# Linear attention with routed experts: kv and the sum of k in one product per two heads, scatters spread over the batch on GpSimd, which also squares the k values

## What is computed

```python
h = layernorm(x) * (1 + ca) + sa
def feature_map(x, orf):                       # x: a head's 8 values, orf: (32, 8)
    proj = x @ orf.T / d_k ** 0.25
    norm = sum(x * x, -1) / (2 * sqrt(d_k))
    return (exp(proj - norm) + EPS) / sqrt(m)  # EPS = 1e-6
q, k = feature_map(h @ Wq.T + bq), feature_map(h @ Wk.T + bk);  v = h @ Wv.T + bv
kv = einsum('nlm,nld->nmd', k, v);  ksum = sum(k, axis=1)
out = (q @ kv) / (q @ ksum)
x = x + ga * (out @ Wo.T + bo)
h = layernorm(x) * (1 + cb) + sb
top1 = argmax(h @ gate_W + gate_b)
x = x + gb * (gelu(h @ W1[top1] + b1[top1]) @ W2[top1] + b2[top1])
```

## Time and profile before

| | us |
|---|---|
| median of three runs | 385.43 (384.46 to 388.31) |
| the profiled execution | 384.86, span 383.1 |
| PE busy in the span | 363.1 (95%) |
| PE weight loads | 281.6 (74%) |
| ACT busy | 278.2 (73%) |
| DVE busy | 271.2 (71%) |
| POOL busy | 202.1 (53%) |

### The profile page before, as it was taken

How to read it: one execution, slowest core, us unless ns; L and a number is a source line. 1 busy time by engine, 2 the same in 40 slices (tenths; PEclk the granted TensorE clock), 3 DMA queues, 4 the chain that set the end, 5 groups by cost and what they waited for, 6 DMA issues and landing times.

```text
span 383.1 us, 13102 instructions
## 1 busy us (share of the span) xinstructions
PE 363.1 (95%) x4547; PEld 281.6 (74%) x4547; DVE 271.2 (71%) x1128; ACT 278.2 (73%) x720; POOL 202.1 (53%) x226
## 2 busy tenths in 40 slices
PE   8899999999999999999999978999989999999990
PEld 7465765766576575657657647999989998999990
DVE  4626787887878779778676879787677775666660
ACT  2588888788888878888888747766656665666650
POOL 2131454854674565657537546546767554555552
PEclk9999999999999999999999999999999999999997
DMA  6496745721321222232122247544565666545310
GB/s 218 175 314 262 248 187 171 226 81 63 113 87 51 93 86 71 74 111 81 47 103 86 71 136 233 159 122 134 167 194 177 188 209 174 165 127 145 89 32 0
DMA packets 30783, 52.38 MB, mean 137 GB/s; under 512 B 4194, under 2 KB 22758, under 8 KB 30336
## 3 DMA queue, kind: packets, MB, share of 16 engines
q1 hardware_dynamic: 24352, 34.50, 30.0%
q0 software_dynamic: 6368, 17.05, 12.2%
HBM read 28.46 MB, written 19.34 MB: 125 GB/s over the span
## 4 chain that ended last, share of the span: by engine, by line
PE 78%; DVE 4%; SPq 3%; issue 3%; ACT 3%; POOL 3%; DMA 3%; DVEq 1%; POOLq 0%; ACTq 0%
PE ps_proj L1247 11%; PE ps_proj L1051 8%; PE ps_feat L1234 6%; PE ps_proj L1084 4%; PE ps_kv L1099 4%; PE ps_feat L1070 4%; PE ps_den L1117 4%; PE ps_kv L1103 4%; PE ps_kv L1131 3%; PE ps_out L1056 3%; PE ps_proj L1087 3%; PE ps_kv L1121 3%; PE ps_feat L1073 3%; PE ps_den L1234 3%; PE ps_kv L1234 3%
## 5 line engine op out<-in xcount | busy, mean ns | idle before, releaser
L484 POOL DMA_INDIRECT out<-kf,modb x71 | 70.7, 995 | 57.3 <-DVE kf L977 50.4
L1247 PE MATMUL ps_proj<-w2sb,qf 128*128 x568 | 74.8, 275 | 0.0
L451 POOL DMA_INDIRECT experts_lists<-pay,slot x64 | 63.8, 997 | 19.1 <-issue 17.4
L1247 PEld LDWEIGHTS ps_proj<-w2sb,qf 128*128 128x128 f32 x568 | 68.9, 192 | 0.2 <-issue 0.2
L613 ACT ACTIVATE xT<-ps_out 128x128 f32<-128x128 f32 x71 | 19.7, 278 | 47.3 <-PE ps_out L1227 47.3
L972 DVE TENSOR_TENSOR kf<-ps_proj,firsts_sb 128x128 f32<-128x128 f32 x71 | 20.7, 291 | 36.2 <-PE ps_proj L1247 25.0
L438 POOL TENSOR_TENSOR wo<-wsb,modb 128x128 f32<-128x128 f32 x16 | 7.6, 475 | 69.2 <-ACT den L591 69.2
L621 ACT ACTIVATE qf<-ps_feat,shared 128x128 f32<-128x128 f32 x144 | 41.0, 376 | 0.0
L1234 PE MATMUL ps_feat<-xT,shared 128*128 128x128 f32 x288 | 38.7, 277 | 1.7 <-issue 0.6
L1234 PEld LDWEIGHTS ps_feat<-xT,shared 128*128 128x128 f32 x288 | 35.0, 192 | 2.9 <-issue 1.6
L1051 PE MATMUL ps_proj<-shared,wsb 128*128 128x512 f32 x62 | 33.4, 620 | 0.3 <-ACT shared L521 0.3
(11 more groups left out here) (187 smaller groups left out, 982.4 us busy)
## 6 DMA issues: line engine op xcount, KB each, us to landing
modb<-experts_lists SPq DMA_DIRECT2D x71, 196.0 KB, 2.5
xall<-in_x SPq DMA_DIRECT2D x16, 256.0 KB, 4.4
pay<-modb SPq DMA_DIRECT2D x16, 256.0 KB, 2.7
modb<-modulation_rows SPq DMA_DIRECT2D x1, 3072.0 KB, 12.1
firsts_sb<-in_firsts SPq DMA_DIRECT2D x1, 2576.0 KB, 10.2
experts_lists<-padding SPq DMA_DIRECT2D x9, 196.0 KB, 2.3
out<-kf,modb POOLq DMA_INDIRECT x71, 2.7
modb<-modulation_rows SPq DMA_DIRECT2D x1, 1024.0 KB, 6.0
```

The lines of the kernel that those rows point to most:

```text
L451: g_.indirect_dma_start(out=lists, in_=pay[b.home][:, t, :], in_offset=None, out_offset=bass.IndirectOffsetOnAxis(ap=slot[b.home][:, t:t + ...
L484: g_.indirect_dma_start(out=rows_out, in_=yb[u], in_offset=None, out_offset=bass.IndirectOffsetOnAxis(ap=token, axis=0), bounds_check=last ...
L1247: ins = mm(Y[u % 2][:, 0:D], g[u % R4][:, c * P:(c + 1) * P], w2sb[:, bass.ds(e * DFF + c * D, D)], start=(c == 0), stop=(c == FC - 1))
```

## The change

- kv and the sum of k come out of one product. The features are laid out by pairs of heads, `kf[:, t, c, j, 0:64]` with the EPS column behind each 64. The stationary operand `v1` has 32 columns for group c and pair j: 16 of v and 16 ones. There are 32 matmuls of 65 columns instead of 16 of 129 and 16 of 128.
- kvT has 128 columns instead of 256 (mask and products 64 wide), so there is one transpose. kvm is copied in two halves of 64 partitions onto a tile that was zeroed.
- kveps is made by TensorE (eight matmuls of one column, ahead of the den product, into bank F[0]) and copied by VectorE between `centre_h2` and `scale_h2`. `k_features` of the next batch waits for that copy, since it writes the same bank.
- ScalarE no longer squares the k values (but for batch 0) and normalises two tiles of each batch; VectorE normalises the other two. `modulate` stands one activation earlier, `k_values` behind `kvm_copy`.
- GpSimd squares the k values (`k_squares(b+1)`), between tile 3 of the scatter of batch b-3 and tile 0 of that of b-2. `gated(b)` follows, then tiles 1 and 2; tile 3 is left for the next batch.

```diff
@@ GpSimd @@
+            g_.memset(kvm[:], 0.0).then_inc(s_kvz, 1)
+            g_.memset(v1[:, :, CW // 2:CW], 1.0).then_inc(s_kvz, 1)
...
+            def k_squares(b):
+
+                pool.wait_ge(s_kst, b.v + 1)
+                g_.tensor_tensor(ksqs, kvals, kvals, ALU.mult).then_inc(s_ksq, 1)
+
...
                 if ahead and b.par == 0:
                     rstd1_of(b.half + 3, b=b + 2)
+                if b.v >= 3:
+                    scatter(b + -3, (3,))
+                if not last:
+                    k_squares(b + 1)
+                if not first and not second:
+                    scatter(b + -2, (0,))
                 gated(b, first)
                 if not first and not second:
-                    scatter(b + -2)
+                    scatter(b + -2, (1, 2))
+                if last:
+                    scatter(b + -2, (3,))
@@ ScalarE @@
             def kvm_copy(b):
                 act.wait_ge(s_kvt, b.v + 1)
-                a.activation(kvm[:], G[:, 0:2 * P], ACT.Copy).then_inc(s_kvm, 1)
+                if b.v == 0:
+                    act.wait_ge(s_kvz, 2)
+                for j in range(2):
+                    half = slice(j * HP, (j + 1) * HP)
+                    a.activation(kvm[half, :, :, j, :], G[half, 0:P].rearrange("p (c n i) -> p n c i", c=NC, n=2),
+                                 ACT.Copy).then_inc(s_kvm, 1)
...
                 k_feature(b, 3)
-                if not first and not last:
-                    normalise1(b + 1, LT // 2, LT)
...
                 q_feature(b, 1)
-                q_feature(b, 2)
                 if not last:
                     modulate(b + 1)
+                q_feature(b, 2)
                 q_feature(b, 3)
+                kvm_copy(b)
                 if not last:
                     k_values(b + 1)
-                kvm_copy(b)
-                if not last:
-                    k_squares(b + 1)
                     q_parts(b + 1)
@@ VectorE @@
-                v.scalar_tensor_tensor(out=kvT[:, 0:P], in0=KV[:, 0:P], scalar=KV[:, P:P + 1], in1=mask,
-                                       op0=ALU.add, op1=ALU.mult, accum_out=kvsum[:, 0:1])
-                v.scalar_tensor_tensor(out=kvT[:, P:2 * P], in0=KV[:, 256:256 + P], scalar=float(L * FEPS), in1=mask,
-                                       op0=ALU.add, op1=ALU.mult, accum_out=kvsum[:, 1:2]).then_inc(s_kvT, 1)
-                dve.wait_ge(s_kvT, b.v + 1)
-                v.tensor_scalar(kveps[:], kvsum[:], FEPS, None, ALU.mult).then_inc(s_eps, 1)
+                for j in range(2):
+                    at = j * (HP + 1)
+                    ins = v.scalar_tensor_tensor(out=kvT[:, j * HP:(j + 1) * HP], in0=KV[:, at:at + HP],
+                                                 scalar=KV[:, at + HP:at + HP + 1], in1=mask,
+                                                 op0=ALU.add, op1=ALU.mult)
+                ins.then_inc(s_kvT, 1)
+
+            def eps_values(b):
+
+                dve.wait_ge(s_epsp, b.v + 1)
+                if b.v:
+                    dve.wait_ge(s_oT, b.v)
+                v.tensor_copy(kveps[:], F[0][:, 0:2]).then_inc(s_eps, 1)
...
+                if not first and not last:
+                    normalise1(b + 1, lo=LT // 2)
                 if not first:
                     residual(b + -1)
                     second_stats(b + -1)
...
                     centre_h2(b + -1)
+                eps_values(b)
+                if not first and not last:
                     scale_h2(b + -1)
@@ TensorE @@
-                pe.wait_ge(s_kst, 2 * (b.v + 1))
+                pe.wait_ge(s_kst, b.v + 1)
+                pe.wait_ge(s_ksq, b.v + 1)
                 if not first:
+                    pe.wait_ge(s_eps, b.v)
...
-                for t in range(LT):
-                    for c in range(NC):
-                        mm(KV[c * CW:(c + 1) * CW, 0:P + 1], v_sb[:, t, c * CW:(c + 1) * CW], kf[:, t, c, 0:P + 1],
-                           start=(t == 0), stop=(t == LT - 1))
-                for t in range(LT):
-                    for c in range(NC):
-                        ins = mm(KV[c * CW:(c + 1) * CW, 256:256 + P], ones32[:], kf[:, t, c, 0:P],
-                                 start=(t == 0), stop=(t == LT - 1))
+                for j in range(2):
+                    for t in range(LT):
+                        for c in range(NC):
+                            ins = mm(KV[c * CW:(c + 1) * CW, j * (HP + 1):(j + 1) * (HP + 1)],
+                                     v1[:, (t * NC + c) * 2 + j, :], kf[:, t, c, j, :],
+                                     start=(t == 0), stop=(t == LT - 1))
                 ins.then_inc(s_kv, 1)
...
+                kv = kvm[:, :, :, :, :].rearrange("p n c j i -> p n c (j i)")
+                for n in range(2):
+                    for c in range(NC):
+                        ins = mm(F[0][c * CW:(c + 1) * CW, n:n + 1], kv[:, n, c, :], kf[:, 0, 0, 0, HP:HP + 1],
+                                 start=True, stop=True)
+                ins.then_inc(s_epsp, 1)
```

68 lines of the change are left out of this document (36 added, 32 removed).

## The result

The changed kernel takes **392.59 us** (median of four runs, 391.52 to 395.26) where the kernel before took 386.32 beside it (384.46 to 388.31): ratio 1.0206, 95% interval 1.0166 to 1.0247. That is slower, clear of the noise, by 1.7 to 2.5 per cent, and by nearly the amount forecast: +7.85 on the profiled execution was predicted (392.7), and the profiled executions stand 6.7 apart (391.52 for 384.86; span 389.7 for 383.1).

A forecast was written before the change was run, and what follows sets the result against it. TensorE, busy throughout 60 to 195, was taken as the bound. With VectorE fully blocked, −0.65 − 0.75 + 4.2 + 5.05 = +7.85 on the profiled 384.86 gave 392.7 us; range 381 to 397.

The forecast's parts named there:

- The product: TensorE's batch: one kv product of about 1.02 replaces the kv product (1.02) and the product with the ones (0.87), gaining 0.87.
- hT: ScalarE's modulation, one activation earlier, ends near 141.5, later than the shorter kv product needs: 0.13 charged per batch.
- The unblocked batch: TensorE's batch if nothing is late: 13.48 − 0.87 − 0.13 + 0.12 + 0.13 = 12.73; whole kernel 381.3, chance 0.25.
- The rival that the product doesn't shrink: 64 loads and passes limit the kv product to 1.9; batch 13.6 without blocking, kernel about 390, or 400 blocked; chance 0.05.
- Full blocking: GpSimd's squares keep VectorE's two-SBUF-input operations out, 0 to 1.28 a batch; batch 13.8, kernel 392.7, chance 0.45.
- the odd batch: Batch without first_moments, with VectorE blocked: centre_h2 ends 1.28 later, k_features 0.82 late, out_project 0.24 more; batch 13.79.
- The even batch: Batch with first_moments: blocked squares end near A+3.05 (A: TensorE starts the attention products), 1.1 late; batch 13.83.
- Start of the batches: Batch 0 gains 0.65 and the interval behind it, without centre_h2, 0.75; 13 more lose 0.32 each.
- The late tile: Tile 3 of batch 12, moved behind rstd2 of batch 14, delays the first expert block's load: 4.25 lost.
- The clock: A TensorE pause of some 5 ahead of the expert blocks may lower the granted clock: first blocks cost up to 2 more.

The follow-up runs named there:

- e1: Changed kernel with k's squares moved from GpSimd back to ScalarE, scatters still spread: 413.61 us, ratio 0.9863 to the kernel before in its group.
- e2: Changed kernel with GpSimd's squares replaced by two memsets of 512 columns, which write but read nothing: 404.83 us, no ratio (one run).
- e3: Changed kernel with GpSimd's squares ahead of tile 3's scatter instead of behind it: 413.57 us, ratio 0.9855 to the kernel before in its group.
- f4: Changed kernel with 76 useless matmuls filling TensorE's wait for the first expert block: 406.27 us, ratio 0.9854 to the kernel before in its group.
- g1: The kernel before, unaltered, traced again on a chip of the experiments: 416.32 us (one run), period 15.02.
- f3: Changed kernel with VectorE's copy of kveps ahead of centre_h2 instead of behind it: 433.73 us, ratio 1.0504 to the kernel before in its group.
- e4: Changed kernel with tile 3 of batch 12 scattered in batch 14's turn, not the last batch: 404.84 us, ratio 0.9636 to the kernel before in its group.
- f1: Changed kernel, unaltered, run again as common base on a chip of the experiments: 404.90 us, ratio 0.982 to the kernel before in its group.
- g2: Changed kernel with squares back on ScalarE, scatters spread, tile 3 of batch 12 issued early: 404.90 us, ratio 0.9645 to the kernel before in its group.

## Why the prediction was right, step by step

- **The product.** Gain 0.87 and 0.13 to pay for hT, so 0.74; measured 1.89 − 1.20 = 0.69. The unblocked batch, 12.73, is 12.80 by the two traces above and 12.81 in the interval without `centre_h2`. The rival that the product doesn't shrink is out.
- **Full blocking** was the likeliest case, and it is what e1, e2 and e3 show. The row that spoke for it in the prediction, L906, is of a copy, which has one SBUF input, and it ended 0.29 behind L445 (229.90 and 229.61); that an operation with two is kept out, these runs are the first to show. The size was off, both ways. The squares take 1.06, not 1.28 (the prediction took the time of L445, an addition of two tiles; that this is the reason is not shown), and lengthen `centre_h2` by 0.79, not by 1.28. So the odd batch is 13.42 where 13.79 was predicted: k_features starts 0.39 late (2.37 for 1.98), not 0.82, and out_project 0.21 late, for 0.24.
- **The even batch** went wrong in its path, and by 0.45: 14.28 for 13.83. I let the squares come in among `scale_h2` and end near A+3.05. They ran from A+1.48 to A+2.53, but VectorE's third operation of `centre_h2`, started at 131.29, was kept out until 133.28, from 0.78 before the squares began. k_features started at A+3.23. That the mean hit is luck, since these two errors cancel: (13.42 + 14.28) / 2 = 13.85 for 13.8.
- **Start of the batches.** The out_projects of the first two batches stand at 28.46 and 40.76 for 28.95 and 41.96, so −0.49 and −1.20, where −0.65 and −1.40 were predicted; at batch 14 the difference is +2.43 (219.65 less 217.22), where the sum had +2.8.
- **The late tile.** Predicted 4.25, and 0.8 more at the end; measured 3.92 (6.35 at the first block less 2.43) and nothing more. The place, rstd2 of batch 14 behind VectorE's work, was right: 225.75, then the tile at 226.99.
- **The clock** was left at nothing in the likeliest case and bounded by 2; f4 shows that it costs. The third block's products start at 240.37 for 232.85, +7.52 where the first block was +6.35: 1.17. Then 0.9 comes back, most of it a pause of TensorE in the trace of before at 319.6 (it waited 0.95 for a load there) that the changed kernel's trace hasn't. So +6.65 at the end: 2.43 + 3.92 + 1.17 − 0.87, where the prediction had 2.8 + 5.05. The clock made up for a part of what the late tile was put too high.
- **What the prediction could not know** is that signals can be held. All its rows come from a trace in which indirect transfers hold nothing. Where the kernel before was traced again, in g1, it loses 1.54 a batch to four scatters in a row (15.02), the changed kernel nothing on the mean (13.79), and the verdict turns: 0.982.

## What to carry to other kernels

Before work is moved to GpSimd, look at what VectorE does at that time: a GpSimd operation that streams from SBUF stopped a VectorE operation with two SBUF inputs until it ended (346 ns became 1131 to 1994), and an engine that was off the path becomes the one waited for. Moving one of them in time moves the collision (f3), so follow what the earlier result releases. A transfer that is moved past a wait must be followed to its last user, here a load three steps on; one exception for the last batch brings the first block 3.9 nearer (e4). And time a change on more than one chip: it was +2.1% in the first comparison and −1.8% on the chip of f1.

## What the runs showed of the hardware that was not expected

- In all four groups of runs, and not in the first comparison, TensorE's signals of finished products arrive late when they fall due while GpSimd issues an indirect transfer: a product due at 142.02 was signalled at 143.2, its scatter's instruction ended at 142.88. In e3 TensorE itself stops once within each k_features, and the group takes 3.05 for 2.07, under a scatter. Whether it belongs to the chip or to the time at which these groups ran is open, and so is what the two engines share. 
- A scatter alone keeps VectorE out by 0.07 at most (e1, 1.13 to 1.20 beside one), nor do the squares alone for longer than 0.79; but with the scatter just ahead of the squares one operation of VectorE was kept for 1994 ns, from before the squares began. Why is open.
- GpSimd's 512-column product of one tile with itself takes 1.04 to 1.10 undisturbed or nearly so, its addition of bog to xall, as many columns from two tiles, 1.28. Which of the differences counts is open.
- A product of 64 records of 65 columns is done in 1.12, one of 16 records of one column takes 0.15 until the next starts.
- The clock fell to 0.50 in the last batch or behind it with a pause (f1) and without (f4, e4, g2), and not there in the kernel before on the first chip. What decides it is open.
